# Two transformer layers in one kernel: keys loaded in halves, work moved between slots, and the second layer's causal mask added by a matmul

## The reference

```python
x = L0_attn_x
xn = _layernorm(x)
x = x + _L0_attn_ref(xn, Wq, Wk, Wv, Wo) + _L0_ffn_ref(xn, W1, b1, W2, b2)      # full attention; gelu, 512 -> 2048 -> 512
xn = _layernorm(x)
x = x + _L1_attn_ref(xn, w_qkv, b_qkv, w_dense, b_dense) + _L1_ffn_ref(xn, w12, b12, w3, b3)
# L1_attn: rotary q and k, scores * 1/16, causal mask (key <= query), softmax; L1_ffn: silu(x1) * x2, 512 -> 2 * 512 -> 512
```

## Time and profile before

| | |
|---|---|
| median of three runs | 607.77 us |
| profiled execution | 603.88 us, span 602.2 us |
| mean granted TensorE clock | 0.997 |
| TensorE busy | 566.0 us (94%) |
| VectorE busy | 456.7 us (76%) |
| ScalarE busy | 348.2 us (58%) |
| POOL busy | 234.2 us (39%) |
| first layer's units | 40 to 376 us, about 21 us each |
| second layer's units | 376 to 594 us, about 14 us each |

### The profile page before, as it was taken

How to read it: one execution, slowest core, us unless ns; L and a number is a source line. 1 busy time by engine, 2 the same in 40 slices (tenths; PEclk the granted TensorE clock), 3 DMA queues, 4 the chain that set the end, 5 groups by cost and what they waited for, 6 DMA issues and landing times.

```text
span 602.2 us, 10503 instructions
## 1 busy us (share of the span) xinstructions
PE 566.0 (94%) x3216; PEld 435.4 (72%) x3216; DVE 456.7 (76%) x1232; ACT 348.2 (58%) x598; POOL 234.2 (39%) x345
## 2 busy tenths in 40 slices
PE   4899899999999999999999998989989999998997
PEld 3797567877777878668777676867667778775764
DVE  6499876856466687476898687798989889789673
ACT  3666746673564673675674666447645664556451
POOL 6143414623203421213223114354745486455242
PEclk9989999999999999999999999999999999999999
DMA  6987442244223244315434314335443354444101
GB/s 199 128 247 226 119 116 81 80 140 109 89 67 107 82 129 124 89 41 170 124 123 123 89 47 130 89 90 129 136 108 87 99 161 130 106 124 113 29 3 70
DMA packets 30535, 67.02 MB, mean 111 GB/s; under 512 B 4880, under 2 KB 18192, under 8 KB 28560
## 3 DMA queue, kind: packets, MB, share of 16 engines
q1 hardware_dynamic: 21840, 38.04, 24.3%
q0 software_dynamic: 8640, 28.32, 15.7%
HBM read 50.87 MB, written 13.63 MB: 107 GB/s over the span
## 4 chain that ended last, share of the span: by engine, by line
PE 69%; DVE 12%; issue 6%; DMA 5%; ACT 5%; POOL 2%; SPq 0%; DVEq 0%; ACTq 0%; POOLq 0%
PE banks L763 47%; PE banks L823 7%; PE banks L849 6%; PE banks L871 6%; DMA q_sb<-max_t 3%; DVE banks L1153 2%; DMA q_sb<-stage 1%; DVE x_res L1197 1%; ACT L1004 1%; DVE hid L1218 1%; PE banks L783 1%; PE banks L852 1%; POOL probs L705 1%; DVE bn L1051 1%; ACT hid_f L1005 1%
## 5 line engine op out<-in xcount | busy, mean ns | idle before, releaser
L985 ACT ACTIVATE probs<-banks 128x512 f32<-128x512 f32 (+1 forms) x256 | 138.0, 545 | 184.9 <-PE banks L849 150.1
L763 PE MATMUL banks<-xnT,w_up 128*128 128x512 f32 x576 | 151.6, 397 | 0.1
L1158 DVE TENSOR_REDUCE neg_max<-banks 128x2 f32<-128x512 f32 x128 | 87.5, 688 | 78.0 <-PE banks L823 76.2
L763 PE MATMUL banks<-w_down,hid 128*128 128x512 f32 x480 | 127.9, 400 | 5.7 <-ACT hid_f L1005 2.0
L763 PEld LDWEIGHTS banks<-xnT,w_up 128*128 128x128 f32 x576 | 101.6, 189 | 27.5 <-issue 10.3
L763 PEld LDWEIGHTS banks<-w_down,hid 128*128 128x128 f32 x480 | 85.3, 189 | 33.4 <-DVE neg_max L1158 8.9
L1153 DVE CUSTOM_DVE_ANT_0 banks<-banks,mask_qk 128x128 f32<-128x128 f32 (+1 forms) x256 | 86.4, 375 | 29.9 <-PE banks L823 29.4
L823 PEld LDWEIGHTS banks<-k_sb,q_sb 96*128 96x128 f32 x512 | 93.1, 193 | 22.0 <-issue 3.4
L823 PE MATMUL banks<-k_sb,q_sb 96*128 96x256 f32 (+1 forms) x512 | 100.4, 278 | 4.2 <-DMA q_sb<-stage 2.0
L705 POOL TENSOR_SCALAR_AFFINE_SELECT probs<-probs 128x256 f32<-128x256 f32 x128 | 61.8, 483 | 78.2 <-ACT probs L985 71.7
L849 PE MATMUL banks<-q_sb,k_sb 97*128 97x512 f32 x192 | 79.2, 412 | 9.9 <-DMA q_sb<-max_t 6.4
(11 more groups left out here) (79 smaller groups left out, 657.1 us busy)
## 6 DMA issues: line engine op xcount, KB each, us to landing
q_sb<-q_parts SPq DMA_DIRECT2D x60, 256.0 KB, 4.4
raw<-in_up POOLq DMA_DIRECT2D x48, 256.0 KB, 3.1
raw<-in_down POOLq DMA_DIRECT2D x40, 256.0 KB, 3.0
q_parts<-stage SPq DMA_DIRECT2D x30, 256.0 KB, 2.5
raw<-in_attn POOLq DMA_DIRECT2D x20, 256.0 KB, 3.6
k_parts<-stage SPq DMA_DIRECT2D x14, 256.0 KB, 2.5
k_sb<-k_parts SPq DMA_DIRECT2D x14, 256.0 KB, 4.0
out<-x_res SPq DMA_DIRECT2D x8, 256.0 KB, 2.2
```

The lines of the kernel that those rows point to most:

```text
L763: mm = nc.tensor.matmul(out_ap, lhs(a), rhs(b_), start=first and j == 0, stop=stop and j == 2, **kw)
L985: nc.scalar.activation(probs[:, i, 0:w], banks[:, ST_BANKS[k % 2], 0:w], ACT.Exp, scale=SCALES[n // B]).then_inc(exp_done, 1)
L1158: nc.vector.tensor_reduce(neg_max[:, s, 2 * g:2 * g + 2, t], banks[:, bank_of[x], :].rearrange("p (r t) -> p r t", r=2)[:, :, 0:w], AX.X, ...
```

## The change

Six edits are made together.

1. The keys of the first batch go to `k_sb` in two halves by key half f. The second half's four DMAs are issued between the first and the second four query DMAs. For this the rows of the first layer's key weights are permuted (f, d, g instead of d, g), and the DRAM layout of its keys with them. ScalarE's wait before it reuses the stage buffer now covers both halves.
2. The four pieces of w_out of the first layer (`attn` 6 to 9), all split in slot 7 of unit 0, are split one by one in slot 7 of units 0 to 3.
3. In the first layer (units 5, 9 and 13) `wo` of the batch before comes behind the eight `up` parts, not ahead of them.
4. In unit 15 the second layer's keys' and values' projection `qkv(5, 2)` comes behind the `up` parts and ahead of `down`, not last.
5. `mt` and `mrow` belong to the head of slot 5, so on every engine they stand ahead of what is due there and of `ctx`.
6. In the second layer, for t = 0, TensorE adds the mask to the scores by a third matmul into the same bank (identity in bf16 by `mask_qk`, now in bf16, repeated for both heads), and VectorE takes one plain maximum over both heads, not negated. For t = 1 the masked maxima stay. VectorE makes the bf16 identity once, in unit 0.

```diff
 RAW = 4
+MT_SLOT = 5
 RING = 3
...
     for g, slot in enumerate(slots):
-        head = [k for k, x in enumerate(slot) if x[0] in ("st", "m")]
+        head = [k for k, x in enumerate(slot) if x[0] in ("st", "m", "mt", "mrow")]
         cut = head[-1] + 1 if head else 0
...
             slots[i].append(("m", u + 2, i - 4))
+        if i == MT_SLOT and u + 1 < UNITS:
+            slots[i] += [("mt", u + 1), ("mrow", u + 1)]
     if s == 2 and n + 1 < 2 * B:
...
         slots[5].append(("ctx", u - 1))
-    if u + 1 < UNITS:
-        slots[5] += [("mt", u + 1), ("mrow", u + 1)]
     slots[5].append(("pv", u, 0))
...
     if s == 3 and n + 2 < 2 * B:
-        fill += parts(("qkv", n + 2, 2))
+        k = 4 if u == LU - 1 else len(fill)
+        fill[k:k] = parts(("qkv", n + 2, 2))
     if s == 0 and 0 < n < 2 * B - 1:
...
     if s == 1 and n > 0:
-        fill = parts(("wo", n - 1, 0)) + parts(("wo", n - 1, 1)) + fill
+        k = 8 if u < LU else 0
+        fill = fill[:k] + parts(("wo", n - 1, 0)) + parts(("wo", n - 1, 1)) + fill[k:]
 
...
         slots[1] += split(0, "down", 2 * u, 2 * u + 1)
-    if u == 0:
-        slots[7] += split(0, "attn", 6, 7, 8, 9)
+    if u < S:
+        slots[7] += split(0, "attn", 6 + u)
     if LU - 6 <= u < LU - 3:
...
         ident = sb("ident", [P, P])
+        identb = sb("identb", [P, P], BF16)
         zero = sb("zero", [P, 1])
-        mask_qk = sb("mask_qk", [P, T])
+        mask_qk = sb("mask_qk", [P, T], BF16)
         bn = sb("bn", [P, NT, 6])
...
         m_loaded = [sem(f"m_loaded{k}") for k in range(RING)]
-        first_k = sem("first_k")
+        first_k = [sem(f"first_k{f}") for f in range(2)]
         first_q = [sem(f"first_q{j}") for j in range(2)]
+        identb_made = sem("identb_made")
         st_filled = sem("st_filled")
...
             if k == 2:
-                eng.wait_ge(first_k, 64)
+                for f in range(2):
+                    eng.wait_ge(first_k[f], 64)
             elif k == 3:
...
                               x_in[b].rearrange("(t p) d -> p t d", p=P)).then_inc(x_loaded[b], 16)
+
+            def first_keys(f):
+                k = stg[("store", 0, 2)]
+                for h in range(2):
+                    for e in range(2):
+                        at = 32 * h + 16 * e
+                        sp_.dma_start(k_sb[at:at + HD, 4 * f:4 * f + 4, :].bitcast(F32),
+                                      stage[64 * f:64 * f + 64, k % 2, h, 0, :].bitcast(F32)).then_inc(first_k[f], 16)
 
...
                     if x == ("store", 0, 2):
-                        for h in range(2):
-                            for e in range(2):
-                                at = 32 * h + 16 * e
-                                sp_.dma_start(k_sb[at:at + HD, :, :].bitcast(F32),
-                                              stage[:, k % 2, h, 0, :].bitcast(F32)).then_inc(first_k, 16)
+                        first_keys(0)
                     elif x == ("store", 0, 0):
...
                                                   stage[:, k % 2, h, j, :].bitcast(F32)).then_inc(first_q[j], 16)
+                            if j == 0:
+                                first_keys(1)
                     elif pair < 2:
...
                         for j in range(2):
-                            dst = kscr[n].rearrange("(h e) d (g t) -> e (d g) h t", e=2, g=NKV)[j]
+                            if n < B:
+                                dst = kscr[n].rearrange("q d x -> q (d x)").rearrange("(h e) (p t) -> e p h t", e=2, t=T)[j]
+                            else:
+                                dst = kscr[n].rearrange("(h e) d (g t) -> e (d g) h t", e=2, g=NKV)[j]
                             sp_.dma_start(dst, stage[:, k % 2, :, 0, :].bitcast(F32)).then_inc(staged[k % 2], 16)
...
                     g = slice(4 * f * T, (4 * f + 4) * T)
+                    if n < B:
+                        src = kscr[n].rearrange("q d x -> q (d x)").rearrange("q (f d x) -> f q d x", f=2, d=HD)[f]
+                    else:
+                        src = kscr[n].rearrange("q d x -> (q d) x")[:, g]
                     sp_.dma_start(k_sb[0:4 * HD, 4 * f:4 * f + 4, :].rearrange("p g t -> p (g t)").bitcast(F32),
-                                  kscr[n].rearrange("q d x -> (q d) x")[:, g]).then_inc(k_loaded[f], 16)
+                                  src).then_inc(k_loaded[f], 16)
                 if x[0] == "mrow":
...
                         else:
-                            pe.wait_ge(first_k, 64)
+                            pe.wait_ge(first_k[f], 64)
                     w = T if n < B or t == 1 else P
...
                                               q_sb[0:ROWS, u % RING, 2 * g + r, t * P:t * P + P], k_sb[0:ROWS, 4 * f + g, 0:w],
-                                              start=r == 0, stop=r == 1, skip_group_check=True)
+                                              start=r == 0, stop=r == 1 and (n < B or t == 1), skip_group_check=True)
+                    if n >= B and t == 0:
+
+                        if x == ("m", LU, 0):
+                            pe.wait_ge(identb_made, 1)
+                        first = banks[:, k, :].rearrange("p (r t) -> p r t", r=2)[:, :, 0:P]
+                        mm = nc.tensor.matmul(first, identb[:, :], mask_qk[:, None, P:].to_broadcast([P, 2, P]),
+                                              start=False, stop=True, skip_group_check=True)
                     mm.then_inc(wk_filled, 1)
...
                     w = T if n < B or t == 1 else P
-                    if n >= B:
+                    if n >= B and t == 1:
 
...
                                             banks[:, bank_of[x], :].rearrange("p (r t) -> p r t", r=2)[:, :, 0:w],
-                                            AX.X, ALU.max, negate=True).then_inc(wk_emptied, 1)
+                                            AX.X, ALU.max, negate=n < B).then_inc(wk_emptied, 1)
+                if x[0] == "bias":
+                    nc.vector.tensor_copy(identb[:, :], ident[:, :]).then_inc(identb_made, 1)
                 if x[0] == "mt":
...
     block = (REP + 2) * HD
-    w0 = np.concatenate([i["L0_attn_Wq"][q_rows(lambda h: h * HD)], i["L0_attn_Wk"][kd(lambda g: g * HD)],
+    k0 = np.array([(4 * f + g) * HD + d for f in range(2) for d in range(HD) for g in range(4)])
+    w0 = np.concatenate([i["L0_attn_Wq"][q_rows(lambda h: h * HD)], i["L0_attn_Wk"][k0],
                          i["L0_attn_Wv"][gd(lambda g: g * HD)]])
...
                             kd(lambda g: g * block + REP * HD), gd(lambda g: g * block + (REP + 1) * HD)])
```

## The result

The changed kernel takes 611.84 us (median of 20 runs) against 607.89 for the kernel before (20 runs), a ratio of 1.0077, 95% interval 1.0055 to 1.0099: 4.7 us slower. Forecast were 599.6 us. The changed kernel's profiled execution has a span of 607.4 us, against 602.2.

The account below looks back on a forecast made before the run. The prediction took TensorE, busy 94% of the span, as the bound. Its terms, 2.7 - 4.0 - 2.5 - 1.7 - 2.7 = -8.2 us, took the median of 607.77 to 599.6, own range 597 to 602, with rivals 592 to 607.

Parts of the forecast that it names:

- step 1: Start: first keys in two halves delay ScalarE's copy and score group 3; a loss of 2.7 us.
- Step 2: Units 0 and 1: one w_out piece per unit instead of four in unit 0; a gain of 4.0 us.
- Steps 3 and 4: w_o behind w_up in units 5, 9, 13: gain 2.5 us; keys' projection ahead of w_down in unit 15: 1.7.
- Step 4: Unit 15: the keys' projection ahead of w_down covers TensorE's pause; a gain of 1.7 us.
- Steps 5 and 6: Mask by matmul with plain maximum, and row of maxima at the head of slot 5: together -2.7 us.
- step 5: Second layer: plain maximum saves VectorE 0.2 us per pair; each added mask matmul costs TensorE 0.12, 7.7 in all.
- (a): Start: the second key half lands in time, so the start gains; 594.8 us, chance 0.12.
- (b): Second layer: the plain maximum saves nothing, 4.2 us less gain; 603.8 us, chance 0.15.
- (c): Second layer: the added matmul doesn't overlap its weight load, 0.48 us each; 619 us, chance 0.07.
- (d): Start costs its upper bound, and units 0 and 1 don't give their gains back; 604.8 us, chance 0.10.
- (e): Second layer gives more, TensorE's whole idle there, 5 us more; 594.6 us, chance 0.12.

Follow-up runs that it names:

- loads_spread: The changed kernel with each first-layer key load issued as four DMAs of 16 partitions: 600.82 us, ratio 0.9892 to the kernel before.
- only_keys: The kernel before with only the first keys in two halves and the key layouts that go with them: 619.43 us, ratio 1.0231.
- only_start: The kernel before with only the keys in two halves, each first-layer key load as four DMAs: 608.20 us, ratio 1.0037.
- only_pad4: The kernel before with first-layer keys in a gapped DRAM tensor, so key loads stay 4 x 16 rows: 616.50 us, ratio 1.0182.
- only_order: The kernel before with only w_o behind w_up in units 5, 9, 13 and unit 15's projection ahead of w_down: 601.51 us, ratio 0.9907.
- only_mask: The kernel before with only the mask added by matmul and the plain maximum: 606.90 us, ratio 0.9993.

## Why the prediction was wrong

**The step that failed is step 1.** It reckoned with edit 1 at the start only, "first keys in two halves: a loss of 2.7 us", and gave the DRAM layout of the keys, which the edit changes as well, no term at all. The start was right: 2.2 us [0.7, 3.8] measured against 2.7, ScalarE's copy at 28.13 against 28, group 3 at 34.50 against 34.55. (1.05 MB at 127 GB/s take 8.3 us and not 8.6, which puts the landing at 27.3 instead of 27.6 and changes little.) What was left out costs five times as much. The first layer's key load turned from 64 equal rows into a pattern whose outermost dimension is 4. The query loads behind it land in up to 10.8 us instead of 7.5, TensorE stands still for some 4 us in units 4 and 8 and then runs at the lower clock. Three comparisons of runs give its price: 11.2 us (the changed kernel against loads_spread), 11.8 (only_keys against only_start) and 11.0 (only_pad4). By the profiles, units 4 and 8 together took 4.9 + 6.6 = 11.5 us more in the changed kernel than in loads_spread.

Without it the change comes out at 0.9892, 601.2 us beside a before of 607.8, inside the forecast's own range of 597 to 602. In part that is luck: edit 2 gave 3 us less than forecast, edits 3 and 4 1.4 more, edit 5 more and edit 6 less, and the errors nearly cancel.

The rule for this was to be had. The Trainium skill (DMA: Bandwidth & Descriptors, Why a DMA increments its semaphore by 16 and not by 1) says that a DMA is shared out over the largest number of engines, up to 16, that divides the slowest dimension of both sides; here that makes 4 instead of 16. The runs agree: the same bytes cost 11 us with a leading 4 and nothing in four parts of 16 rows, and at the end of each wait of the changed kernel, only_pad4 and only_keys the busy share of the DMA engines is 0.17 to 0.31, about 4 of 16. Which engines carried the key load no view shows.

The fixed 2.0 us of the prediction's step 1 stand in the Trainium skill (DMA: Bandwidth & Descriptors, Anatomy of one DMA) for DMAs that GpSimd issues. The DMAs of step 1 are SyncE's, so that figure bears on them only loosely; the sum did without it.

**Step 2**: right in kind and too large, with 4.0 forecast. Unit 1 gave 5.1 in the changed kernel with TensorE gapless, but 1.2 came back in units 2 and 3, and alone the edit is worth 1.0 [-0.5, 2.7]. The three subtractions were costed as hidden; the units that take the pieces got longer, and more of the gain is missing than that.

**Steps 3 and 4**: right, with 4.2 forecast together and 5.6 [3.7, 7.6] measured. No wait for the hidden activations is left in units 5, 9 and 13. Step 4 has no run of its own, and only_order's profile gave its gain back in unit 16.

**Steps 5 and 6** (edits 6 and 5): -2.7 forecast together. Edit 5 alone gave 4.6, by the lengths of the units most of it in the first layer, where the prediction had no gain: units 2, 6, 10, 12 and 14 are 0.3 to 0.9 us shorter, and TensorE's waits for the turned normalized input, 0.29 at most, are gone from units 2, 6, 10 and 14. The prediction spoke of that order for the stretch with unit 20 alone. Edit 6 gave about nothing.

Two prices of step 5 were misread. These rows are the changed kernel's, by line and shape, then in order of time:

```profile
L1184 DVE TENSOR_REDUCE neg_max<-banks 128x2 f32<-128x256 f32 x64 | 26.7, 417 | 17.0 <-PE banks L850 16.6
...
L850 PE MATMUL banks<-mask_qk,identb x64: 283/285/288, 356.5 to 575.6; 128*128 128x256 bf16 x64
...
453.75 0.42 DVE L1184 TENSOR_REDUCE neg_max<-banks 128x2 f32<-128x256 f32 x1
454.09 0.68 DVE L1246 TENSOR_TENSOR hid<-hid_f,hid 128x512 fp32r<-128x512 f32 x1
```

The plain maximum is shown with 0.417 against the 0.42 forecast, and the next operation starts 0.34 behind it. But the pair of masked maxima that it replaces took 0.47 from start to start (0.46 in the mean of the pairs with no wait behind them), not 0.57. So VectorE gains 0.13 per pair and not 0.2, 8 us in all 64 instead of 13; its busy time fell by 5.6 us in the changed kernel and by 8.8 in only_mask. On TensorE the mask matmul costs 0.08 in most places and not 0.12.

What failed most is the sentence that VectorE "gives 5.4 of TensorE's 6.5 idle" in 376 to 452. Units 16 to 20 gained 1.3. TensorE's 2.5 us of waits for the row went there, and its waits for masked maxima grew from 1.2 to 2.0, now all for the other block of queries, which the edit leaves as they were:

```profile
391.81 0.41 PE L842 MATMUL banks<-k_sb,q_sb 96*128 96x128 f32 x2 [0.99 <-DVE neg_max L1179]
```

VectorE's relief lies in slots 4 to 7, where the first block's maxima stand, and this wait in slots 0 to 3. That is read from the trace of the changed kernel; no run moved the relief into those slots.

**The rivals.** (a), the start gains, is excluded by 28.13 and by the start's loss of 2.2. (b), the plain maximum saves nothing, is near the truth in its sum, since edit 6 gained 0.4 us [-1.5, 2.2] alone, but not in its mechanism: VectorE did save time, and TensorE could use little of it. (c), the added matmul doesn't overlap its weight load, is excluded: it costs 0.08 to 0.12 and not 0.48. (d) is excluded by the start's 2.2 us, at most 3.8. (e), more from the second layer, isn't seen: its units took 1.4 us more in the profile. No rival named the key load.

## What to carry to other kernels

When an edit changes a layout, list every DMA that reads or writes the tensor and write down the outermost dimension of both sides before and after; six transfers of the same bytes went from harmless to 11 us. Look then at what is in flight beside and behind it and not only at the transfer itself: here the profile had no landing time for the key load, and what showed that it was slow were its longer issue, the late landing of the loads behind it and of POOL's beside it, and a low busy share of the DMA engines while TensorE waited. Price an operation from start to start on both sides of the change, not from its shown duration. An operation made cheaper helps only in the slots in which somebody waits for it, so read off the slot of the wait before crediting the saving.

## What the runs showed of the hardware

- Six key loads of 256 KB whose pattern has to stay 4 x 16 rows cost the kernel 11 us in 607 and are issued in 0.585 us each instead of 0.49; written 4 x 16 at one regular distance they land in 4.0 us as with 64 rows; as four DMAs of 64 KB each the median is 2.4 us to landing.
- In the last 3 us of TensorE's waits behind these loads the busy share of the 16 DMA engines was 0.17 to 0.31, and two loads on POOL's own queue took 7.7 us to landing instead of 2.9 to 3.0.
- After 4.04 us of standing still TensorE ran the next ten 512-column matmuls in 4.47 us instead of about 2.5, at a granted clock of 0.50, so a DMA wait of 4 us cost over 6. After a wait of 3.34 us in unit 4 of only_keys the clock stayed at 1.00, after one of 3.45 in its unit 8 it was 0.50.
- A bf16 matmul of 256 columns that adds to sums of float32 products is shown with 285 ns and costs TensorE 0.08 us ahead of a large product and 0.12 ahead of the small turning matmul. Left out of a stretch of 83 us in which TensorE is nearly always busy, 24 of them gave 1.3 us.
- Two masked maxima of 128 columns with their accumulator reads take VectorE 0.46 us from start to start, one plain maximum over 2 x 128 columns 0.34.
